# Batch 0's first q and k groups by direct copies, extra matmuls in the prologue, and a new order of row-maximum and reciprocal steps

## What is computed

```python
def _ada_rmsnorm(x, t, gamma_w, beta_w):
    gamma = (t @ gamma_w.T)[:, None, :]
    beta = (t @ beta_w.T)[:, None, :]
    return gamma * _rmsnorm(x) + beta
...
q = split(x @ W_q.T)
k = split(x @ W_k.T)
v = split(x @ W_v.T)
attn = jax.nn.softmax(scale * jnp.einsum('bnqd,bnkd->bnqk', q, k), axis=-1)
o = jnp.einsum('bnqk,bnkd->bnqd', attn, v)
o = o.transpose(0, 2, 1, 3).reshape(b, l, dm)
return o @ W_o.T
...
x = x + a_alpha * _attention(_ada_rmsnorm(x, t, attn_gamma_w, attn_beta_w), W_q, W_k, W_v, W_o)
f_alpha = (t @ ffn_alpha_w.T)[:, None, :]
return x + f_alpha * _swiglu(_ada_rmsnorm(x, t, ffn_gamma_w, ffn_beta_w), gate_w, hidden_w, out_w, out_b)
```

## Time and profile before

| what | value |
|---|---|
| median of 3 runs | 777.21 us (777.11 to 779.03) |
| profiled execution | 781.7 us |
| its span | 779.9 us |
| PE busy | 721.0 us, 92% |
| DVE, ACT, POOL busy | 69%, 60%, 50% |
| mean granted TensorE clock | 0.976 of full |

### The profile page before, as it was taken

One profiled execution on the slowest core, in us unless ns is written; L12 is line 12 of the kernel. 1 busy time (PEld: TensorE's weight loads), 2 busy tenths in 40 slices (PEclk: granted clock), 3 DMA queues, 4 the chain that ended last, 5 costly groups with the idle time before them and its releaser, 6 DMA issues.

```text
span 779.9 us, 17477 instructions
## 1 busy us (share of the span) xinstructions
PE 721.0 (92%) x6646; PEld 489.3 (63%) x6646; DVE 536.2 (69%) x795; ACT 470.8 (60%) x858; POOL 392.1 (50%) x493
## 2 busy tenths in 40 slices
PE   5678787899999999999999999999999999999995
PEld 4333233455676767675676667776677667679895
DVE  3576675678667776777667776768667776536765
ACT  4347574778566756667666756667666655753431
POOL 4335331345248553666348553766447453872433
PEclk9769998999999999999999999999999999999998
DMA  6855655445442644445442553445443440242110
GB/s 193 270 176 182 203 189 166 163 124 210 132 165 68 202 144 148 140 137 183 132 164 80 192 162 131 137 137 158 137 157 102 172 141 15 58 116 64 49 50 28
DMA packets 63676, 108.75 MB, mean 139 GB/s; under 512 B 10240, under 2 KB 17848, under 8 KB 63592
## 3 DMA queue, kind: packets, MB, share of 16 engines
q1 hardware_dynamic: 62760, 106.78, 43.0%
q10 hardware_dynamic: 704, 0.66, 0.3%
q0 software_dynamic: 128, 0.20, 0.1%
HBM read 59.60 MB, written 39.09 MB: 127 GB/s over the span
## 4 chain that ended last, share of the span: by engine, by line
PE 69%; DVE 9%; DMA 8%; issue 6%; ACT 4%; SPq 3%; POOL 1%; ACTq 0%; POOLq 0%; DVEq 0%
PE ps_x L1323 16%; PE ps_j L1210 11%; PE ps_o L1296 11%; PE ps_j L1336 9%; PE ps_s L1283 9%; PE ps_m L1270 6%; DVE mx L1030 4%; DMA out_scratch<-o_raw 2%; PE ps_o L1336 2%; ACT prob L837 2%; DVE fx L996 2%; DMA qs<-m_hl 1%; DVE gate_t L1070 1%; PE ps_m L1323 1%; DMA prob<-in_wk 1%
## 5 line engine op out<-in xcount | busy, mean ns | idle before, releaser
L1030 DVE TENSOR_REDUCE mx<-ps_m 128x2 f32<-128x1024 f32 x222 | 271.6, 1223 | 126.4 <-PE ps_m L1270 125.9
L837 ACT ACTIVATE prob<-ps_s 128x1024 f32<-128x1024 f32 x256 | 262.0, 1024 | 82.4 <-PE ps_s L1283 81.8
L1283 PE MATMUL ps_s<-qs,ks 64*128 64x512 f32 x512 | 120.4, 466 | 21.5 <-ACT prob L837 15.0
L1296 PE MATMUL ps_o<-prob,v 128*32 128x512 f32 x1024 | 139.0, 615 | 0.2 <-ACT o_raw L845 0.2
L1283 PEld LDWEIGHTS ps_s<-qs,ks 64*128 64x128 f32 x512 | 48.7, 186 | 141.0 <-issue 73.8
L1270 PE MATMUL ps_m<-ks,qs 64*128 64x512 f32 x444 | 94.0, 419 | 9.3 <-DVE mx L1030 5.6
L1323 PE MATMUL ps_x<-n,gh_hi 64*128 64x256 f32 x872 | 97.8, 284 | 1.6 <-DVE act_y L1077 1.6
L554 POOL TENSOR_TENSOR a_lo<-act_y,a_hi 128x256 fp32r<-128x256 f32 x100 | 73.7, 737 | 46.5 <-ACT a_hi L868 46.3
L1323 PE MATMUL ps_x<-n_x,gh_hi 64*128 64x256 f32 x872 | 94.3, 276 | 0.0
L579 POOL TENSOR_TENSOR xr<-xr,sc 128x512 f32<-128x512 f32 x41 | 53.3, 1300 | 63.1 <-DVE sc L1042 40.6
L1323 PEld LDWEIGHTS ps_x<-n,gh_hi 64*128 64x128 f32 x872 | 74.3, 184 | 13.6 <-DVE act_y L1077 10.1
(11 more groups left out here) (176 smaller groups left out, 1439.6 us busy)
## 6 DMA issues: line engine op xcount, KB each, us to landing
qs<-stack_scratch SPq DMA_DIRECT2D x31, 512.0 KB, 5.1
ks<-stack_scratch SPq DMA_DIRECT2D x31, 512.0 KB, 6.4
stack_scratch<-qk_hi SPq DMA_DIRECT2D x56, 256.0 KB, 3.2
out_scratch<-o_raw SPq DMA_DIRECT2D x32, 256.0 KB, 2.9
n_x<-n SPq DMA_DIRECT2D x32, 256.0 KB, 3.7
stack_scratch<-qk_lo SPq DMA_DIRECT2D x28, 256.0 KB, 3.5
on_lo<-out_scratch SPq DMA_DIRECT2D x16, 256.0 KB
d_c<-reciprocal_scratch SPq DMA_DIRECT2D x16, 256.0 KB
```

The costliest lines, as they stand in the source:

```text
L837: act.activation(prob[:, n % 2, 2 * h:2 * h + 2, :], ps_s[:], ACT.Exp, scale=SCALE).then_inc(p_r, 1)
L1030: dve.tensor_reduce(mx[:, group % 2, :, h, qt], max_pair(mp)[:], AX.X, ALU.max).then_inc(mx_red, 1)
L1283: mm = pe.matmul(ps_s[:, s, :], ks[r:r + 64, g, j, kb * P:(kb + 1) * P], qs[r:r + 64, g, j, :], start=True, stop=True)
L1296: mm = pe.matmul(ps_o[32 * i:32 * i + 32, :], v[:, g, kb, i, :], prob[:, n % 2, i, :], start=(kb == 0), stop=(kb == TT - 1), skip_group_ch ...
```

## The change

**Batch 0, groups 0 and 1.** The weights of q and k are arranged anew for the first half: the stationary block of group g holds 64 columns of q and 64 of k (`w_first`), in the space that the feed-forward weights `gh_hi` and `gh_lo` take later. One projection then gives q of a group in partitions 0 to 63 and k in 64 to 127. The number of projection matmuls is the same. `stack_direct` copies high and low parts straight from the staging tile (`n2`, printed as `n`) into `qs` and `ks`: per group 12 DMAs of 32 partitions by 512 (64 KB each), 6 per pair, with no DRAM scratch between. The 6 writes and 6 reads of the first two groups go. The fourth rows of batch 0's `qs` and `ks` come from two new DMAs at the start (`row_pads`). The counts `writes` and `reads` follow from this.

**Weights.** ACT and DVE now split the rearranged first-half weights in two pieces of 256 columns, and the full q and k weights, which the second half and all later batches need, a second time: ACT after the normalised input, DVE between the low parts of group 0 and group 1. PE's second half waits for it.

**Unread matmuls.** `warm_up` adds 3, 3 and 4 matmuls of the identity with itself into `ps_m`, whose result nothing reads: before the coefficient product, before the transposes, and before the first projection.

**Order.** `o_read(0, 0)` moves from unit 9 to 10, behind `max_rows(0, 3)`; its reciprocal from 11 to 12, `rec_write` and `rec_read` from 11 to 13, `o_norm` from 13 to 15, `o_high` and `o_low` from 14 to 15. `o_read(0, 1)` moves from unit 17 to 18, behind `max_rows(1, 1)`; its reciprocal from 18 to 19, `rec_write` and `rec_read` from 19 to 20 and behind `stack_write(2, 0)`, `o_norm` from 20 to 21, `o_high` and `o_low` from 21 to 22.

```diff
+        def writes(b, q):
+
+            return 4 * b + q - 2
+
+        def reads(b, g):
+
+            return b - (g < 2)
+
+        def w_first(w, k):
+
+            return w[:, 0, 2 * P * k:2 * P * (k + 1)].rearrange("p (g i n) -> p g i n", g=2, i=2)
+
+        def w_first_raw(k):
+
+            return w_raw[:, k, 0:2, 0:P].rearrange("p i (g n) -> p g i n", g=2)
...
-            for c in range(2):
+            for dst, pad in ((qs, zeros), (ks, d_c[:])):
+                rows = dst[3::4, 0:2].rearrange("p g j n -> p (g j) n").bitcast(F32)
+                sp.dma_start(rows, pad[0:P // 4].unsqueeze(1).broadcast_to([P // 4, NG, T])).then_inc(row_pads, 16)
+
+            for c in (1, 0):
                 for i, pad in enumerate((zeros, d_c[:])):
                     rows = stack_d[i, c].rearrange("j (r t n) -> (j r) t n", t=4, n=T)
...
-            def stack_read_pairs():
-
-                sp.wait_ge(scr_w, 48 * 2)
-                sp.wait_ge(pad_written, 64)
-                for j, arrived in enumerate((pair_in, stack_in[0])):
+            def stack_direct(g):
+
+                sp.wait_ge(qk_lo_r, g + 1)
+                hi, lo = (a.bitcast(F32) for a in qk_stage(0, g))
+                for j in range(2):
                     for i, dst in enumerate((qs, ks)):
-                        src = stack_d[i, 0, j].rearrange("(r n) -> r n", n=T)
-                        sp.dma_start(dst[:, 0, j].bitcast(F32), src).then_inc(arrived, 16)
-
-            stack_write(0, 0)
-            stack_write(0, 1)
-            stack_read_pairs()
-            stack_read(0, 1)
+                        r = 64 * i + 32 * j
+                        for t, src in enumerate(((hi, lo, hi), (hi, hi, lo))[i]):
+                            sp.dma_start(dst[t::4, g, j].bitcast(F32), src[r:r + 32]).then_inc(direct_in[g][j], 16)
+
+            stack_direct(0)
+            stack_direct(1)
...
-                if at(1, -1):
+                if at(1, -1) and b > 1:
...
+                if n == UNITS + 2:
+                    o_read(0, 1)
+                if at(3, -1) and b > 1:
                     rec_write(b - 1, 1)
                     rec_read(b - 1, 1)
+                if at(3, -1):
                     load_xr(b - 1, 1)
                 if at(3, 1):
                     stack_write(b + 1, 0)
+                if n == UNITS + 4:
+                    rec_write(0, 1)
+                    rec_read(0, 1)
...
-                if at(9, 0):
+                if at(9, 0) and b > 0:
...
+                if n == 10:
+                    o_read(0, 0)
+                if at(11, 0) and b > 0:
...
+                if n == 13:
+                    rec_write(0, 0)
+                    rec_read(0, 0)
...
-                if at(4, -1):
+                if at(5 if b == 1 else 4, -1):
...
-                if at(13, 0):
+                if at(15 if b == 0 else 13, 0):
...
-            act.wait_ge(wqk_in, 32)
-            act.activation(w_hi[:, :, 0:2], w_raw[:, :, 0:2], ACT.Copy).then_inc(w_hi_r, 1)
             act.wait_ge(job_full, JOB_NO["COEF", 0, 0])
             act.activation(coef[:, 0:2].rearrange("p i k b -> p (i k b)"), ps_o[:, 0:2 * KC * B], ACT.Copy).then_inc(coef_r, 1)
+            act.wait_ge(wqk_in, 32)
+            for k in range(KC):
+                act.activation(w_first(gh_hi, k), w_first_raw(k), ACT.Copy).then_inc(w_hi_r, 1)
             act.wait_ge(coef_r, 1)
             y_high(0, 0, ps_j[:])
             y_high(0, 1, ps_g)
             act.wait_ge(wvo_in, 32)
-            for dst, src in ((w_hi[:, :, 2], w_raw[:, :, 2]), (wo_hi[:], w_raw[:, :, 3])):
+            for dst, src in ((w_hi[:, :, 0:2], w_raw[:, :, 0:2]), (w_hi[:, :, 2], w_raw[:, :, 2]), (wo_hi[:], w_raw[:, :, 3])):
...
-                if at(5, -1):
+                if at(6 if b == 1 else 5, -1):
                     o_high(b - 1, 1)
-                if at(14, 0):
+                if at(15 if b == 0 else 14, 0):
...
-            w_low(1, w_lo[:, :, 0:2], w_hi[:, :, 0:2], w_raw[:, :, 0:2])
+            for k in range(KC):
+                w_low(k + 1, w_first(gh_lo, k), w_first(gh_hi, k), w_first_raw(k))
...
+                if q == 1:
+                    w_low(KC + 1, w_lo[:, :, 0:2], w_hi[:, :, 0:2], w_raw[:, :, 0:2])
...
-                if at(2, -1):
+                if at(3 if b == 1 else 2, -1):
                     o_recip(b - 1, 1)
-                if at(11, 0):
+                if at(12 if b == 0 else 11, 0):
...
-                    pe.wait_ge(pair_in, 32)
-                elif mp == 1 or (qt == 0 and j == 0):
-                    pe.wait_ge(stack_in[g], 32 * (b + 1))
+                    pe.wait_ge(row_pads, 32)
+                if b == 0 and g < 2:
+                    if qt == 0:
+                        pe.wait_ge(direct_in[g][j], 96)
+                elif qt == 0 and j == 0:
...
+            def warm_up(times):
+
+                for _ in range(times):
+                    pe.matmul(ps_m[:, 0, 0:P], ident[:], ident[:], start=True, stop=True)
+
+            pe.wait_ge(consts, 6)
+            warm_up(3)
             pe.wait_ge(small_in, 16 * 3)
             coefficients(0, ps_o)
-            pe.wait_ge(consts, 6)
+            warm_up(3)
             transposes(0, 0, ps_j)
             transposes(0, 1, ps_g)
-            pe.wait_ge(w_lo_r, 1)
+            warm_up(4)
+            pe.wait_ge(w_lo_r, KC)
             for k in range(KC):
                 pe.wait_ge(n_hi_r, k + 1)
-                for q in range(2):
+                for g in range(2):
                     for a in range(2):
-                        pe.matmul(ps_s[:, q], W[a][:, k, q, 0:P], n_hi[:, k, :], start=(k + a == 0), stop=False)
+                        pe.matmul(ps_s[:, g], W_FIRST[a][:, k, g, :], n_hi[:, k, :], start=(k + a == 0),
+                                  stop=False)
             pe.wait_ge(n_lo_r, 2)
-            for q in range(2):
+            for g in range(2):
                 for k in range(KC):
-                    mm = pe.matmul(ps_s[:, q], w_hi[:, k, q, 0:P], n_lo[:, k, :], start=False, stop=(k == KC - 1))
+                    mm = pe.matmul(ps_s[:, g], W_FIRST[0][:, k, g, :], n_lo[:, k, :], start=False,
+                                   stop=(k == KC - 1))
                 mm.then_inc(job_full, 1)
+            pe.wait_ge(w_lo_r, KC + 1)
```

40 lines of the change are left out of this document (22 added, 18 removed).

## The result

The kernel after takes 772.01 us (median of 11 runs, 770.18 to 775.76), the kernel before beside it 779.49 us (776.51 to 780.95). The ratio is 0.9917, 95% interval 0.9898 to 0.9935: 7.5 us faster. The forecast was 765.6 us, with a range of 762.0 to 771.5. The sign was right, the median lies 0.5 us above the range, and it lies 6.4 us above the forecast. Of these, 4.1 us are gain that did not come (7.5 for 11.6), and 2.3 us are the starting point: the forecast began at 777.21 us, the median of three runs, and eleven runs give 779.49.

The account below looks back on a forecast made before the run. PE's own work was taken to bound the main part, leaving waits in the front: 4.0 (unit 12) + 5.5 (unit 20) + 2.1 (prologue) = 11.6 us, from the 777.2 us median to 765.6, range 762 to 771.5.

Parts of the forecast that it names:

- What bounds the kernel: Main part: PE's own work alone counts, so whatever the front gains before unit 28 should stay to the end.
- Units 12 and 20: PE's waits for row-maximum copies held behind SP, plus low clock after them: gains of 4.0 and 5.5 us.
- residual of 0.3 us: Wait for the row-maximum copies expected to remain at each of units 12 and 20, from 0 to 0.8 us.
- The step that failed: Whole sum: 11.6 us read from a 781.7 us profiled execution was subtracted from the 777.2 us median.
- The prologue: Start to unit 0: DVE's second row maximum at 29.9 instead of 31.99, gain 2.1 us, ends 0.6 and 3.1.
- its lower end: Prologue: clock falls again while PE waits for the weights, projections and tables run slower; a loss of 1.5 us.
- The direct copies: Prologue: group 0's 12 copies at 0.5 us issue and 3.25 us landing arrive by 27.5, ahead of the tables.
- The rule that the prediction cites: Small DMAs should be merged, under 64 KB is mostly overhead; by it the 24 copies would be dear.
- The rival built on SP's issue cost: Prologue: small copies at up to 1.28 us per issue delay unit 0's scores; slower, 783 us, chance 0.05.
- The reciprocal steps: Batch 0's reciprocal chains, moved later, stay under PE's work; cost 0 to 1 us, taken as 0.
- The prologue gains nothing: Rival: unread matmuls delay the projection, clock stays low, PE waits for weights; 767.5 to 771 us, chance 0.18.
- The clock rises early and holds: Rival: max scores and units 0 and 1 run at the full clock; 761 to 764 us, chance 0.13.

## Why the prediction was wrong in size and right in kind

- **What bounds the kernel** was right: from unit 28 to unit 127 all 19 profiles have 527.9 to 528.2 us. What the front gains is kept there. It is not kept to the end: the stretch behind unit 127 took back 3.2 us in the mean of four profiles, and the prediction had no term for it.
- **Units 12 and 20** were read rightly. SP's order was the cause; with the copies ahead the waits are gone, even the residual of 0.3 us each. In the profiled pair unit 11 to unit 24 became 10.06 us shorter, for 9.5 in the sum: 3.99 from unit 11 to 13 (forecast 4.0) and 5.90 from unit 19 to 21 (forecast 5.5). That unit 12's part is not over 4.0 without the residual has a reason that the sum left out. With a wait in front and at the full clock unit 12 takes 3.95 us, as unit 4 does; without the wait it takes 4.36, since PE then waits 0.34 us for ACT within it.
- **The step that failed** is the sentence "the gain is in waits that every run has, so I take it from the median". Every profiled run has the waits, but not of this length, and not the low-clock spells behind them: the two places cost 10.2 us in the first profile and 6.4 in the mean of four, and units 11 to 24 took 56.5 to 60.4 us, the first profile being the dearest. The order is worth 6.8 and 7.2 us by the medians of its two sessions. The prediction had the sign of this before it: a profiled execution of 781.7 us against runs of 777.11 to 779.03. A gain that removes a wait of varying length removes the profile's excess too. It belongs to the profiled time, or must be scaled down before it is taken from a median. (Counted from the profiled time it gives 770.1 us, and the profiled execution of after took 770.18. That is luck in part, since this execution was the lowest of eleven, without the late write of the tail.) With the 7.2 us of the table in place of 9.5, the forecast would have been 777.2 − 7.2 − 2.1 = 767.9 us. The other 4.1 us are the prologue's 2.1, which the medians don't show, and the starting point, 2.3 us too low with three runs; together these are slightly more than the difference.
- **The prologue** (2.1 us, ends −1.5 and 3.1) measured 1.0 in the profiled pair, 0.4 over four profiles each, and nothing by the medians. Up to PE's second half it was well placed: the last unread group ends at 13.42 (forecast 13.0 to 13.8), SP lets go at 17.67 (18.2), and the second half starts at 18.83 (18.26 + 1.2 = 19.5). What was mis-sized is the second half itself: the clock fell behind the gap, the case that the text named only as its lower end. It made the second half's matmuls last from 18.83 to 23.28 us and not to 21.75, that is 1.5 us. The first unread group, ahead of the coefficients, was given no price; it shows only against the kernels without it, where the second half mostly starts 1.0 us sooner. Tables were out at 30.07 (29.71 + 0.36) for a forecast of 29.1, DVE's second maximum at 31.00 for 29.9, and from there to unit 0 both kernels take the same 13.23 us.
- **The direct copies** were hidden, as forecast: 24 issues of 0.59 us in the median (forecast 0.5), landing 2.0 to 2.8 us later (forecast 3.25). The rule that the prediction cites from the Trainium skill, "DMA: Bandwidth & Descriptors", section "Rules for kernel authors", agrees with the trace in SP's part, where 64 KB cost 0.59 us and 256 KB 0.45. It did not decide the time, since PE waited for the tables and never for these copies. The rival built on SP's issue cost needed 1.09 us each.
- **The reciprocal steps** at nothing: right. PE waits nowhere for `on_lo` from 84 to 155 us.
- **The rivals.** "The prologue gains nothing" is the one that came true by the medians. Its reasons are in the trace in part: the first projection begins later than before (13.42 against 13.03) and PE waits 2.08 us for the weights, but the clock doesn't stay low, it falls behind that wait. With its own range of 767.5 to 771 it would still have been too low, for the other reason. "The clock rises early and holds" is half true: the first projection runs at 0.23 us a matmul in every profile with the ten, but from 30 to 50 us the granted clock is 0.50, as before.
- **Not in the sum at all**: the late write in the tail, some 3 us in the profiles that have it. It was not to be seen in the trace of before, and its cause stays open.

The fastest version tried has the new order and the direct copies, none of the ten unread matmuls, and eight in the gap: 769.49 and 770.25 us (ratios 0.9878 and 0.9879), against 772.01, 774.12 and 772.08 for the kernel after. The filled gap itself is not shown by the medians: with the gap idle the same kernel took 770.85 and 771.02.

## What to carry to other kernels

A wait behind a queue that races a DMA has a length that changes from execution to execution. Before its price is taken from one trace, compare that trace's own time with the timed runs, and look at a second profile. If the profile is the dear one, scale the price down. Unread matmuls paid here where PE was idle in any case and nothing useful stood behind them: nine in each of two waits were worth 2.9 us of 779.6. In front of a step on the path they hold it up. Ten of them in the prologue moved PE's second half by 1.0 us in most profiles, and in no session was the kernel with them clearly the faster one.

## What the hardware showed beyond expectation

- A landing 3.3 us earlier (83.86 against 87.13, with unit 11 at 84.21 and 86.76, so 0.7 us beyond the shift), and copies that took 0.6 us less, changed the wait at unit 12 from 2.96 to 1.66 us, and the low-clock spell behind it was missing altogether.
- A wait of 1.76 us at unit 12 was followed by a spell of 1.53 us in one execution, and one of 1.66 us by none in another.
- At the very start the spacing of the matmuls tells more than the clock record. From 10 to 17 us the granted clock reads 1.00 in the profiles with and without the ten, while the matmuls of the first projection stand 0.43 us apart in some and 0.23 in others.
- The same idle gap of 2.08 us was followed by a low spell in one execution (0.66 over 20 to 25 us) and not in another (1.00) of the same kernel.
- One write of 256 KB, issued about 8.06 us after unit 127, landed after 2.0 to 2.3 us in 15 profiles and after 3.6 to 4.5 in four.
- Copies of 64 KB from one tile to every fourth partition of another cost SP 0.59 us each, and landed in 2.1 us in the median.
